# Wide cross attention in a Perceiver kernel: another order of the work of one batch

## The chip, the cores and the metric

The kernel runs on one core of a Trainium2 chip. The metric is device time in microseconds for one launch, the median of several executions. A batch is one of 32 independent rows of the input.

## What is computed

The program is a two-layer Perceiver. Its fourth stage, the one that changes, is the second cross attention: 64 latent queries of each of 32 batches attend to 1601 context rows with 16 heads of 16 dimensions.

```
q = (x @ Wq).reshape(B, N, 16, 16)          # B=32, N=64
k = (context @ Wk).reshape(B, M, 16, 16)    # M=1601, context dim 192
v = (context @ Wv).reshape(B, M, 16, 16)
scores = einsum('bhid,bhjd->bhij', q, k) * scale
scores = where(context_mask, scores, max_neg)
attn = softmax(scores)
out = einsum('bhij,bhjd->bhid', attn, v)
```

The output projection comes in the next stage.

## The kernel before

`wide_cross_attention` (L1550) computes keys and values of one batch from the transposed context in chunks, takes the row maxima of the scores in one pass, and in a second pass computes the scores again with keys on the partitions, exponentiates them and multiplies them with the values. Keys lie in 13 tiles of 124 (the last one shorter) and in four chunks of 4, 3, 3 and 3 tiles.

The work is a software pipeline over batches. In iteration n the rounds of `ROUNDS` (L1611) run in the order written there, and every engine walks the same list (`schedule`, L1641) and does its own part of each round. Rounds in `OF_B` work on batch n, those in `OF_NEXT` on batch n+2, `F1` and `F2` on batch n-1, all others on batch n+1. The first two and the last two batches are unrolled, and the loop between holds 28 batches. The rounds are:

- `K c`: key projection of chunk c, two halves of 5 matmuls (L1907). ScalarE rounds a copy to khi (L1831), VectorE copies the exact keys to kf (L2014).
- `V0 c`, `V1 c`: value projection of chunk c, up to two tiles each. ScalarE copies to val (L1859).
- `A c` (16 of them): rough scores for the maxima, two row-tiled matmuls (L1936) with a chunk's columns. VectorE adds the mask and takes the maximum (L2029).
- `mred`: VectorE joins the maxima and negates them (L2038 to L2041). `M`: TensorE transposes them (L1942), ScalarE copies them to augq (L1848).
- `B c` (13 of them): scores of key tile c, 12 row-tiled matmuls (L1956, L1959), which need augq. After every second tile ScalarE exponentiates two tiles (L1867). The score bank holds one pair, so an even tile waits for both exponentials of the pair before.
- `PV c`: 16 column-tiled matmuls (L1976) of the exponentials with the values into acc. `F0` copies acc to accs (ScalarE, L1873). `F1` multiplies accs by a selector (L1988), and ScalarE takes a logarithm and an exponential of the result for the reciprocal (L1877, L1879). `F2` multiplies and stores (L2047, stores at L1763).
- `Ln`, `X` on SyncE: loads of the context (L1727). `Sn`/`S`: ScalarE splits it (L1822, L1823). `Xn`/`X`: VectorE's rest (L2006 to L2008).
- `Q2`: VectorE scales the queries (qs, L2017). Behind this, SyncE loads the mask and the queries of the next batch, which is batch n+2 (L1731, L1736, 9 DMAs). `Qn`: ScalarE counts the mask with mcopy (L1837), GpSimd makes the mask's bias from the count. `Q1n`: ScalarE's rounded queries (L1842).

K, V, A, M and F1 share three PSUM banks, ring0 to ring2, in turn. `FILLS` (L1622) lists the fills in order of rounds, with 51 places; a fill waits until the one three places before it has been read by its last reader (`room`, L1887): for K that is VectorE's kf copy, for V ScalarE's, for A VectorE's maximum, for F1 the logarithm.

Of the kernel before, what the change touches and what calls it, by code (L numbers as in the profile page):

```python
# [378 lines left out]
def latent_cross_attention(nc, consts, ctx_x, ctxT, mask, g, b, WkvT, qT, klT, vl, oT):  # L379
# [15 lines left out]
    with ExitStack() as ctx:  # L395
# [65 lines left out]

        ROUNDS = [("R", 0), ("K", 1), ("Q", 0), ("B", 0), ("X", 3), ("RS", 1),
# [13 lines left out]
        FILLS = []  # L476
        for kind, c in ROUNDS:
            if kind in ("K", "Kn"):
# [21 lines left out]
        def schedule(engine_step, loop_engine, chain=None, per_round=0):  # L500

            def one(n, s):
                for kind, c in ROUNDS:
                    if kind in OF_B:
                        if there(n):
                            engine_step(kind, c, n, s % 6)
                    elif kind in OF_LAST:
                        if there(n - 1):
                            engine_step(kind, c, n - 1, (s + 5) % 6)
                    elif kind in OF_NEXT:  # L510
                        if there(n + 2):
                            engine_step(OF_NEXT[kind], c, n + 2, (s + 2) % 6)
                    elif there(n + 1):
                        engine_step(kind, c, n + 1, (s + 1) % 6)
# [1035 lines left out]
def wide_cross_attention(nc, consts, ctxT, mask, Wkv, qT, oT):  # L1550
# [17 lines left out]
    with ExitStack() as ctx:  # L1568
# [14 lines left out]
        kf = m.sbuf("kf", [128, 2, 2, W2])  # L1583
        val = m.sbuf("val", [128, 2, NKT, NH, VW])
# [11 lines left out]
        augq = m.sbuf("augq", [128, 2, 256], BF16)  # L1596
# [11 lines left out]
        sc = m.psum("sc", [128, 4, 512])  # L1608
        acc = m.psum("acc", [128, 256])

        ROUNDS = [("Ln", 0), ("Ln", 1), ("A", 0), ("B", 0), ("A", 1), ("B", 1), ("A", 2), ("X", 2), ("K", 1), ("F1", 0), ("PV", 0),  # L1611
# [6 lines left out]
        OF_B = ("B", "PV", "F0")  # L1618
        OF_NEXT = {"Ln": "L", "Sn": "S", "Xn": "X", "Kn": "K", "Qn": "Q", "Q1n": "Q1"}

        FILLS = []  # L1622
        turn = ROUNDS.index(("Kn", 0))
        for kind, c in ROUNDS[turn:] + ROUNDS[:turn]:
            if kind in ("Kn", "K"):
                FILLS += [(("K", c, o), "kf", 8, 2 * c + o, 0) for o in range(2)]
            elif kind == "V0":
                FILLS += [(("V", c, 0), "val", 8, 2 * c, 0)]
            elif kind == "V1":
                FILLS += [(("V", c, 1), "val", 8, 2 * c + 1, 0)]  # L1630
            elif kind == "A":
                FILLS += [((kind, c, o), "maxed", 32, 2 * c + o, 0) for o in range(2)]
            elif kind == "M":
                FILLS += [((kind, c, 0), "augq", 1, 0, -1)]
            elif kind == "F1":
                FILLS += [((kind, c, 0), "lden", 1, 0, -2)]
        while len(FILLS) % len(ring):
            FILLS.append(None)
        PLACE = {f[0]: n for n, f in enumerate(FILLS) if f}
# [1 line left out]
        def schedule(engine_step, loop_engine, chain=None, per_round=0):  # L1641

            def one(n, p, do_a, do_b, do_next, do_f):
                for kind, c in ROUNDS:
                    if kind in OF_B:
                        if do_b:
                            engine_step(kind, c, n, p)
                    elif kind in ("F1", "F2"):
                        if do_f:
                            engine_step(kind, c, n - 1, 1 - p)  # L1650
                    elif kind in OF_NEXT:
                        if do_next:
                            engine_step(OF_NEXT[kind], c, n + 2, p)
                    elif do_a:
                        engine_step(kind, c, n + 1, 1 - p)
# [909 lines left out]
def perceiver(nc, a, out):  # L2565

    N, D = a["x"].shape
    E = a["wg"].shape[1]
    slots = E * (int(N / E * 1.25) + 1)

    def scratch(name, shape):
        return nc.dram_tensor(name, shape, F32, kind="Internal").ap()
    qT, klT, oT0, q3T, oT3 = (scratch(name, (D, N)) for name in ("qT", "klT", "oT0", "q3T", "oT3"))
    vl, x2, x4, xn = (scratch(name, (N, D)) for name in ("vl", "x2", "x4", "xn"))
    logits = scratch("logits", (N, E))
    buf, ybuf = scratch("buf", (slots, D)), scratch("ybuf", (slots, D))

    latent_projections(nc, a, a["x"], a["ln_l_g"], a["ln_l_b"], a["qn_g"], a["kn_g"], a["WqT"], a["WlkvT"], qT, klT, vl)
    latent_cross_attention(nc, a, a["ctx"], a["ctxT"], a["mask0"], a["ln_x_g"], a["ln_x_b"], a["WkvT"], qT, klT, vl, oT0)
    gated_attention_and_ffn(nc, a, a["x"], oT0, a, x2, q3T)  # L2580
    wide_cross_attention(nc, a, a["ctxT"], a["mask1"], a["Wkv3"], q3T, oT3)
    laplacian_attention_and_router(nc, a, x2, oT3, a, x4, xn, logits, buf)
    routed_experts(nc, a, x4, xn, logits, a, buf, ybuf, out)
# [46 lines left out]
```

## Time and profile before

| | |
|---|---|
| median of 3 runs | 3820.42 us (3816.07 to 3820.52) |
| profiled execution | 3818.75 us, its span 3817.0 us |
| TensorE matmul | busy 3019.8 us, 79% |
| VectorE | busy 2548.8 us, 67% |
| ScalarE | busy 1931.1 us, 51% |
| GpSimd | busy 748.6 us, 20% |

The changed stage runs from about 1896 to 3282 us of the span. Times in the rows are microseconds from the start of the span, unless marked ns. A row of the order of time has start, duration (of several merged instructions together), engine, line, operation, what is written and read, count, and in brackets the idle time before it with what ended it. PE is TensorE, PEld its weight loads, DVE is VectorE, ACT is ScalarE, SPq the queue of SyncE. L12 is line 12 of the kernel.

### The profile page before, as it was taken

Reading aid. Unit: us, or ns where it says so; the run is one execution under the profiler, and the core shown is the slowest. Engines: PE = TensorE matmul, PEld = TensorE weight load, DVE = VectorE, ACT = ScalarE, POOL = GpSimd, SP = SyncE. Lnnn points to the kernel's source line nnn. Section 1 sums busy time; section 2 is a strip of 40 time slices with the busy share of each in tenths; the row PEclk is TensorE's granted clock in tenths of the full one; section 3 lists DMA queues with packets and bytes.
Section 4 is the critical chain, followed back from the end, with each engine's and each line's share of the span. In section 5 each row is a group of like instructions: output and inputs, shape, how many; then the busy total and the mean of one; then the engine's idle time right before and its main releaser. Section 6 shows DMA issues by size and latency. Waiting matters only on the chain. (4 is left out here: it accounts for less than half of the span.)

```text
span 3817.0 us, 103916 instructions
## 1 busy us (share of the span) xinstructions
PE 3019.8 (79%) x36990; PEld 2570.1 (67%) x36990; DVE 2548.8 (67%) x7485; ACT 1931.1 (51%) x4178; POOL 748.6 (20%) x836
## 2 busy tenths in 40 slices
PE   3449999999999985566379999999999999543674
PEld 3348888888888884444258788787888888432453
DVE  5568888888888854766567777776777777464000
ACT  1146666667666643333236666666666666321111
POOL 0223233332333310000132211211221221001001
PEclk7669999999999996777569999999999999765887
DMA  2123332323323302000111111111111111213411
GB/s 65 52 85 81 82 83 81 81 82 82 83 81 80 84 10 66 23 22 17 37 33 40 42 42 40 42 40 39 43 39 43 43 39 27 77 41 111 156 48 61
DMA packets 235455, 221.58 MB, mean 58 GB/s; under 512 B 69516, under 2 KB 228545, under 8 KB 234816
## 3 DMA queue, kind: packets, MB, share of 16 engines
q1 hardware_dynamic: 232896, 208.22, 19.4%
q0 software_dynamic: 2048, 6.68, 0.5%
q8 instruction: 304, 4.98, 0.5%
q14 instruction: 207, 1.70, 0.1%
HBM read 186.30 MB, written 28.39 MB: 56 GB/s over the span
## 5 line engine op out<-in xcount | busy, mean ns | idle before, releaser
L1867 ACT ACTIVATE xb_P<-xb_sc 124x1024 f32<-124x1024 f32 (+1 forms) x416 | 405.6, 1023 | 428.9 <-PE xb_sc L1959 428.9
L2029 DVE CUSTOM_DVE_ANT_0 xb_junk<-xb_ring,xb_mbias 128x372 bf16<-128x372 f32 (+2 forms) x1024 | 526.3, 571 | 102.9 <-PE xb_ring L1936 98.6
L1936 PE MATMUL xb_ring<-xb_khi,xb_qhi 32*128 32x372 f32 (+2 forms) x1024 | 405.5, 443 | 45.4 <-DVE xb_kf L2014 16.0
L879 PE MATMUL xa_acc<-xa_raw,xa_P 124*128 124x193 f32 x1664 | 315.6, 330 | 7.3 <-ACT xa_P L754 7.0
L1959 PE MATMUL xb_sc<-xb_qs,xb_kf 32*124 32x128 f32 x6656 | 317.3, 271 | 0.0
L2014 DVE COPY xb_kf<-xb_ring 128x372 f32<-128x372 f32 (+2 forms) x256 | 138.8, 572 | 244.8 <-ACT xb_khi L1831 239.8
L1907 PE MATMUL xb_ring<-xb_xst,xb_whi 128*128 128x372 f32 (+2 forms) x768 | 263.2, 370 | 43.6 <-DVE xb_xst L2008 38.0
L1907 PE MATMUL xb_ring<-xb_whi,xb_xst 128*124 128x256 f32 (+1 forms) x1248 | 286.4, 292 | 2.9 <-DVE xb_maxes L2029 0.4
L1936 PEld LDWEIGHTS xb_ring<-xb_khi,xb_qhi 32*128 32x128 f32 x1024 | 181.3, 185 | 153.1 <-DVE xb_maxes L2029 56.4
L1959 PEld LDWEIGHTS xb_sc<-xb_qs,xb_kf 32*124 32x124 f32 x6656 | 282.7, 182 | 0.0
L879 PEld LDWEIGHTS xa_acc<-xa_raw,xa_P 124*128 124x128 f32 x1664 | 266.4, 189 | 18.7 <-ACT xa_P L754 12.3
L1804 POOL TENSOR_SCALAR xb_augk<-xb_mask,xb_some 1x1602 bf16<-1x1602 uint8 x128 | 206.4, 1613 | 252.6 <-PE xb_sc L1959 236.0
L865 PE MATMUL xa_sc<-xa_qblk,xa_kT 128*124 128x128 f32 x1664 | 239.0, 272 | 0.0
L1976 PE MATMUL xb_acc<-xb_P,xb_val 124*17 124x64 f32 x13312 | 230.8, 220 | 4.2 <-ACT xb_P L1867 4.2
L1907 PEld LDWEIGHTS xb_ring<-xb_whi,xb_xst 128*124 128x124 f32 (+1 forms) x1248 | 216.8, 188 | 22.7 <-DVE xb_maxes L2029 15.9
L672 POOL CAST xa_kTr<-xa_kT 128x744 fp32r<-128x744 f32 (+1 forms) x128 | 109.9, 858 | 621.2 <-ACT xa_kT L740 621.2
L1976 PEld LDWEIGHTS xb_acc<-xb_P,xb_val 124*17 124x17 f32 x13312 | 190.7, 97 | 44.0 <-issue 15.7
L1907 PE MATMUL xb_ring<-xb_wlo,xb_xst 128*124 128x256 f32 (+1 forms) x832 | 218.3, 284 | 0.0
L865 PEld LDWEIGHTS xa_sc<-xa_qblk,xa_kT 128*124 128x124 f32 x1664 | 216.1, 187 | 0.1
L1956 PE MATMUL xb_sc<-xb_augq,xb_augk 32*124 32x256 bf16 (+1 forms) x1664 | 201.3, 303 | 1.6 <-ACT xb_P L1867 1.6
L1907 PEld LDWEIGHTS xb_ring<-xb_xst,xb_whi 128*128 128x128 f32 x768 | 146.5, 193 | 76.7 <-issue 43.0
L1907 PE MATMUL xb_ring<-xb_xst,xb_wlo 128*128 128x372 f32 (+2 forms) x512 | 180.2, 352 | 0.0
(430 smaller groups left out, 7720.8 us busy)
## 6 DMA issues: line engine op xcount, KB each, us to landing
xa_raw<-in_ctx SPq DMA_DIRECT2D x64, 279.0 KB
ex_w<-in_W SPq DMA_DIRECT2D x16, 1024.0 KB, 10.1
xa_raw<-in_ctx SPq DMA_DIRECT2D x32, 372.0 KB
xa_xTr<-in_ctxT SPq DMA_DIRECT2D x64, 186.0 KB, 2.5
xb_raw<-in_ctxT SPq DMA_DIRECT2D x64, 186.0 KB, 2.5
xa_xTr<-in_ctxT SPq DMA_DIRECT2D x32, 248.0 KB, 2.7
xb_raw<-in_ctxT SPq DMA_DIRECT2D x32, 248.0 KB
xa_mask<-in_mask SPq DMA_DIRECT2D x32, 200.1 KB, 5.3
```

What stands on the lines that cost most here:

```text
L672: nc.gpsimd.tensor_copy(kTr[:, c % 2, :, 0:W], kT[:, p, :, k0:k0 + W]).then_inc(sem("kTr"), 1)
L865: i = nc.tensor.matmul(s_[0:w, 256 * u + 128 * o:256 * u + 128 * o + 128], kt[:, o, :], qblk[:, t3, o, :], start=False, stop=True, skip_gr ...
L879: i = nc.tensor.matmul(acc[:, o, :], w, raw[0:KEYS, t3, t, :], start=t == 0 and o == 0, stop=t == NKT - 1, skip_group_check=True)
L1804: nc.gpsimd.tensor_scalar(augk[r:r + 1, p, :], mask8[r:r + 1, :], -1.0, some[r:r + 1, 1:2], ALU.add, ALU.mult).then_inc(sem("augk"), 1)
L1867: nc.scalar.activation(P[0:w, pbuf(t, p), :].rearrange("p (r n) -> p r n", r=4), sc[0:w, :, half], ACT.Exp).then_inc(sem("exped"), 1)
L1907: i = nc.tensor.matmul(out, l, r, start=k == 0, stop=k == 4)
L1936: i = nc.tensor.matmul(bank[:, 0:w], qhi[r, p, o, 128 * s:128 * s + 128], khi[r, p, o, k0:k0 + w], start=True, stop=True)
L1956: nc.tensor.matmul(sc[0:w, r, at:at + 256], augk[rows(r), p, keys], augq[rows(r), p, :], start=True, stop=True)
L1959: i = nc.tensor.matmul(sc[0:w, r, at + 128 * o:at + 128 * o + 128], kf[rows(r), p, o, keys], qs[rows(r), p, o, 128 * (r % 2):128 * (r % 2) ...
L1976: i = nc.tensor.matmul(acc[32 * j:32 * j + VW, 64 * g:64 * g + 64], val[0:w, p, c, h, :], P[0:w, pbuf(c, p), place(h):place(h) + 64], star ...
L2014: v.tensor_copy(kf[:, p, o, k0:k0 + w], ring[f % 3][:, 0:w]).then_inc(sem("kf"), 1)
L2029: v.tensor_tensor_reduce(out=junk[:, k, 0:w], in0=ring[f % 3][:, 0:w], in1=mbias[:, p, k0:k0 + w], scale=1.0, scalar=-3.0e38, op0=ALU.add, ...
```

## The change

The list `ROUNDS` is put in another order. It has the same rounds and no instruction is added or removed on any engine. In the new list A2, X2 and K1 stand between B1 and B2, nothing between B2 and B3, and A3 follows; most A rounds stand alone or in pairs between other rounds where they stood in groups of three; PV rounds stand singly in the first half; F1 stands ahead of A1; Q2 stands behind K3 instead of ahead of A5; Qn stands behind A14; mred and M stand ahead of Kn, and Sn2 is last. Since M and others now lie on the other side of the point where the list of fills begins (`turn`), the offsets in `FILLS`, which say of which batch a fill is relative to the others, are computed by a function `behind` instead of being written out.

```diff
-        ROUNDS = [("Ln", 0), ("Ln", 1), ("A", 0), ("B", 0), ("A", 1), ("B", 1), ("A", 2), ("X", 2), ("K", 1), ("F1", 0), ("PV", 0),
-                  ("A", 3), ("B", 2), ("A", 4), ("B", 3), ("S", 3), ("K", 2), ("V0", 0), ("F2", 0), ("Q2", 0), ("PV", 1), ("PV", 2),
-                  ("A", 5), ("B", 4), ("A", 6), ("B", 5), ("A", 7), ("X", 3), ("V1", 0), ("V0", 1), ("PV", 3), ("PV", 4),
-                  ("A", 8), ("B", 6), ("A", 9), ("B", 7), ("A", 10), ("Sn", 0), ("K", 3), ("V1", 1), ("Qn", 0), ("PV", 5), ("PV", 6),
-                  ("A", 11), ("B", 8), ("A", 12), ("B", 9), ("Xn", 0), ("Sn", 1), ("V0", 2), ("V1", 2), ("PV", 7), ("PV", 8),
-                  ("A", 13), ("B", 10), ("A", 14), ("B", 11), ("A", 15), ("Sn", 2), ("V0", 3), ("V1", 3), ("mred", 0), ("PV", 9), ("PV", 10),
-                  ("B", 12), ("Q1n", 0), ("Xn", 1), ("Kn", 0), ("M", 0), ("PV", 11), ("PV", 12), ("F0", 0)]
+        ROUNDS = [("Ln", 0), ("Ln", 1), ("A", 0), ("B", 0), ("F1", 0), ("A", 1), ("B", 1), ("A", 2), ("X", 2), ("K", 1), ("B", 2),
+                  ("B", 3), ("A", 3), ("K", 2), ("V0", 0), ("PV", 0), ("A", 4), ("PV", 1), ("S", 3), ("A", 5), ("B", 4), ("A", 6),
+                  ("PV", 2), ("A", 7), ("B", 5), ("PV", 3), ("A", 8), ("V1", 0), ("F2", 0), ("A", 9), ("B", 6), ("B", 7), ("X", 3),
+                  ("A", 10), ("V0", 1), ("PV", 4), ("Sn", 0), ("PV", 5), ("A", 11), ("K", 3), ("Q2", 0), ("Sn", 1), ("V1", 1), ("PV", 6),
+                  ("PV", 7), ("A", 12), ("B", 8), ("B", 9), ("A", 13), ("V0", 2), ("A", 14), ("Qn", 0), ("PV", 8), ("PV", 9), ("A", 15),
+                  ("B", 10), ("B", 11), ("V1", 2), ("V0", 3), ("V1", 3), ("Xn", 0), ("mred", 0), ("B", 12), ("PV", 10), ("Xn", 1),
+                  ("M", 0), ("Q1n", 0), ("Kn", 0), ("PV", 11), ("PV", 12), ("F0", 0), ("Sn", 2)]
...
-        for kind, c in ROUNDS[turn:] + ROUNDS[:turn]:
+
+        def behind(kind, n):
+
+            return (-2 if kind in OF_B else -3 if kind in ("F1", "F2") else 0 if kind in OF_NEXT else -1) + (n < turn)
+
+        for at in range(turn, turn + len(ROUNDS)):
+            kind, c = ROUNDS[at % len(ROUNDS)]
+            d = behind(kind, at % len(ROUNDS))
```

## Rows read from the trace of the kernel before

**Rows 1.** Stretches of TensorE: stretch, length, PE busy (count), clock, DMA, GB/s

```profile
2389.57:2430.87 41.30, 39.79 (x830) 1.00 0.15 41
2389.57:2392.89 3.32, 3.11 (x58) 1.00 0.02 5
2409.08:2411.69 2.61, 2.40 (x53) 1.00 0.11 22
2426.48:2427.17 0.69, 0.69 (x27) 1.00 0.00 0
```

**Rows 2.** Waits from 2300 to 3300: us in total, times, longest

```profile
PEld xb_ring L1936 <- DVE xb_maxes L2029: 39.0, 119, 0.6
PEld xb_ring L1936 <- DVE xb_kf L2014: 31.0, 87, 0.7
```

**Rows 3.** Order of time of TensorE in one batch

```profile
2400.47 0.28 PE L1907 MATMUL xb_ring<-xb_whi,xb_xst 128*124 128x256 f32 x1
...
2401.74 1.09 PE L1976 MATMUL xb_acc<-xb_P,xb_val 124*17 124x64 f32 x64
2402.76 0.61 PE L1936 MATMUL xb_ring<-xb_khi,xb_qhi 32*128 32x372 f32 x2
...
2410.30 0.43 PE L1936 MATMUL xb_ring<-xb_khi,xb_qhi 32*128 32x372 f32 x1 [0.18 <-DVE xb_maxes L2029]
...
2411.69 0.43 PE L1907 MATMUL xb_ring<-xb_xst,xb_whi 128*128 128x362 f32 x1
...
2413.46 0.28 PE L1907 MATMUL xb_ring<-xb_whi,xb_xst 128*124 128x256 f32 x1
...
2427.17 0.49 PE L1907 MATMUL xb_ring<-xb_xst,xb_whi 128*128 128x496 f32 x1
...
2429.53 0.38 PE L1942 MATMUL xb_ring<-xb_ident,xb_negmax 128*128 128x128 f32 x2
...
2430.87 0.70 PE L1936 MATMUL xb_ring<-xb_khi,xb_qhi 32*128 32x496 f32 x2
```

**Rows 4.** Order of time of VectorE in the same batch

```profile
2390.37 0.68 DVE L2029 CUSTOM_DVE_ANT_0 xb_junk<-xb_ring,xb_mbias 128x496 bf16<-128x496 f32 x1 [0.56 <-PE xb_ring L1936]
...
2394.06 0.54 DVE L2006 TENSOR_TENSOR xb_xst<-xb_raw,xb_xst 64x372 fp32r<-64x372 f32 x1
...
2395.74 1.00 DVE L2014 COPY xb_kf<-xb_ring 128x372 f32<-128x372 f32 x2
...
2403.13 0.48 DVE L2017 TENSOR_SCALAR xb_qs<-xb_qf,xb_some 128x512 f32<-128x512 f32 x1
...
2409.69 0.55 DVE L2029 CUSTOM_DVE_ANT_0 xb_junk<-xb_ring,xb_mbias 128x372 bf16<-128x372 f32 x1 [1.64 <-PE xb_ring L1936]
...
2410.16 0.54 DVE L2029 CUSTOM_DVE_ANT_0 xb_junk<-xb_ring,xb_mbias 128x372 bf16<-128x372 f32 x1
...
2424.89 0.17 DVE L2041 SCALAR_TENSOR_TENSOR xb_negmax<-xb_most,xb_neghi 128x8 f32<-128x8 f32 x1
```

**Rows 5.** Order of time of ScalarE in the same batch

```profile
2405.24 1.94 ACT L1867 ACTIVATE xb_P<-xb_sc 124x1024 f32<-124x1024 f32 x2 [2.54 <-PE xb_sc L1959]
...
2414.23 0.81 ACT L1831 ACTIVATE xb_khi<-xb_ring 128x362 fp32r<-128x362 f32 x2
...
2415.20 1.53 ACT L1837 ACTIVATE xb_mcopy<-xb_mask 128x1602 bf16<-128x1602 uint8 x1
```

**Rows 6.** SyncE's queue: query loads at the start, mask and queries in the loop

```profile
1904.85 3.70 SPq L1736 DMA_DIRECT2D xb_qf<-q3T  x8
...
2446.68 0.37 SPq L1731 DMA_DIRECT2D xb_mask<-in_mask  x1
2447.24 4.53 SPq L1736 DMA_DIRECT2D xb_qf<-q3T  x8
```

**Rows 7.** DMA issues from 2300 to 3300: count, size, median us to landing

```profile
xb_raw<-in_ctxT SPq DMA_DIRECT2D x44, 186.0 KB, 2.4
...
oT<-xb_o_sb SPq DMA_DIRECT2D x100, 16.0 KB, 1.5
```

More of the change, by code:

```diff
@@ L1623, in wide_cross_attention @@
         turn = ROUNDS.index(("Kn", 0))
-        for kind, c in ROUNDS[turn:] + ROUNDS[:turn]:
+        def behind(kind, n):
[3 more added lines that the diff above has]
+            d = behind(kind, at % len(ROUNDS))
             if kind in ("Kn", "K"):
-                FILLS += [(("K", c, o), "kf", 8, 2 * c + o, 0) for o in range(2)]
+                FILLS += [(("K", c, o), "kf", 8, 2 * c + o, d) for o in range(2)]
             elif kind == "V0":
-                FILLS += [(("V", c, 0), "val", 8, 2 * c, 0)]
+                FILLS += [(("V", c, 0), "val", 8, 2 * c, d)]
             elif kind == "V1":
-                FILLS += [(("V", c, 1), "val", 8, 2 * c + 1, 0)]
+                FILLS += [(("V", c, 1), "val", 8, 2 * c + 1, d)]
             elif kind == "A":
-                FILLS += [((kind, c, o), "maxed", 32, 2 * c + o, 0) for o in range(2)]
+                FILLS += [((kind, c, o), "maxed", 32, 2 * c + o, d) for o in range(2)]
             elif kind == "M":
-                FILLS += [((kind, c, 0), "augq", 1, 0, -1)]
+                FILLS += [((kind, c, 0), "augq", 1, 0, d)]
             elif kind == "F1":
-                FILLS += [((kind, c, 0), "lden", 1, 0, -2)]
+                FILLS += [((kind, c, 0), "lden", 1, 0, d)]
         while len(FILLS) % len(ring):
```

## The prediction, made before the change was run

> **What bounds the kernel now.** The change touches one stage of six. The first view to read is the table of stretches: one batch of this stage, from the first maxima matmul of one batch to that of the next, takes 41.30 us and TensorE is counted busy for 39.79 us of it, at a granted clock of 1.00, the 2.4 GHz level [rows 1]. So TensorE, which walks the hand-written order, sets the period; the clock has nothing left to give. The second view is the list of waits: in 1000 us the weight loads waited 39.0 us for the maxima (VectorE L2029) and 31.0 us for the key copies (L2014) [rows 2]. Both are waits for one of the three ring banks. The third view is the order of time on TensorE. A8 begins at 2409.08 [rows 1], the second matmul of A9 has to wait until 2410.30 and K3 starts only at 2411.69 [rows 3]: this group of three A and two B rounds takes 2.61 us [rows 1]. VectorE explains it: its first reduction starts at 2409.69, the second at 2410.16, so one follows each 0.47 us [rows 4], and the fourth, which frees K3's bank, is over at about 2411.6. Three A rounds in a burst want 2.8 us of VectorE and TensorE has far less to do meanwhile. The group A0 to A2 with its 496 columns takes 3.32 us for the same reason [rows 1]. A lone B takes 0.69 us [rows 1]. If A costs 0.3 us and B 0.6 us unstalled, a group of 3 A and 2 B would need 2.1 us, so some 0.5 to 1.2 us of each such group is stall (there are six a batch, of which the rows show two): 3 to 5 us a batch is the most that any order can win here. It is more than the 1.5 us of idle time in the table, because a stalled pair of matmuls runs one behind the other and is counted busy.
>
> **The steps that cost nothing or little.** No instruction is added or removed; all is order. M with its copy goes ahead of K0: two transposes of 0.38 us together [rows 3], whose negated maxima are ready if VectorE has passed A15, X0 and the reduction; between A15 and M TensorE now has B10, B11, V12, V03, V13, B12 and PV10, about 5 us, against some 4 us on VectorE (two reductions 0.9; X0, 2.2, which is X2's 1.68 [rows 4] at 496 columns; the maxima's four small operations, of which the last took 0.17 [rows 4], 0.8). Cost nothing; if the cover failed, below 0.5 us. F1 goes ahead of A1, and A2 now waits for its bank until ScalarE took the logarithm; behind F1 stand A1 and B1, and that covers it. Sn2 goes behind F0: its 0.8 us of ScalarE lies in a place where it idled, and its reader X2 comes 5 us later. S3, Sn0, Sn1 and both Xn are moved among copies that have a microsecond of slack; Sn1 now stands ahead of V11's copy and waits about 0.2 us for V11's matmuls, with only that copy behind it. On SyncE the stores of F2 stay behind X2's loads, and X3's two loads now run before Q2's nine instead of behind them. GpSimd's chain hangs on ScalarE's Q and on the last B round, and has half a batch of slack.
>
> **The maxima.** I walk the new order with the old durations, t from A0, each A's second matmul and each next ring user waiting for the bank three places back. Durations: a reduction 0.47 us (0.6 at 496 columns), first one 0.6 to 0.8 us after its matmul, X2 1.68, a key copy 0.5 [rows 1, 3, 4]; K 1.8 (K3 took 1.77), V00 1.27, two PV 1.02, K0 2.36 [rows 3]; an isolated A 0.35 (not shown; bounds: 0.2, a bare pair of passes, and 0.46, A10 to K3 with a wait in it [rows 3]; I take the middle); F1 0.6, an estimate from M, whose two matmuls are half as wide. A0, B0, F1 to 1.8; A1 to 2.15, B1; A2 2.7 and, waiting, 3.3; K1 3.9 to 5.6; B2, B3 to 6.75. Here is the stall that stays: VectorE needs 0.8 + six reductions to 5.0, then X2 to 6.7, then K1's copies to 7.7, so A3 is held until 7.3 and K2 until 7.8. K2 to 9.6, V00 to 10.8, PV0, A4, PV1 to 12.2; A5 (0.4 of waiting), B4, A6 (0.4), PV2, A7, B5, PV3 to 15.7; A8, V10 to 17.35; A9, B6, B7, A10, V01 to 20.3; PV4, PV5 to 21.35; A11 (0.35 of waiting, behind X3), K3 21.95 to 23.65. Before, K3 ended 23.89 us after A0 (2413.46 less 2389.57) [rows 1, 3], with PV5 and A11 (0.9 us) still to come. Gain to this point: 1.1 us.
>
> From there on, stalls are few: V11, PV6, PV7, A12 to A13 with B8 and B9, V02, A14, PV8, PV9, A15 with B10 and B11, V12, V03, V13 end at about 34.1. Then B12 0.69 [rows 1], PV10 0.51, M 0.32 (1.34 from M to A0 less two PV), K0 2.36, PV11 and PV12 1.02 [rows 3]: 4.9 us, so A0 would follow at 39.0, a gain of 2.3 us a batch.
>
> **The load that comes due.** Q2 is the step that I think decides. On VectorE it scales the queries (L2017, 0.48 us [rows 4]); then SyncE may load the mask and the queries of the batch after next, nine DMAs, and ScalarE's mcopy (Qn, L1837, 1.53 us [rows 5]) waits for them. Before, Q2 ended at 2403.6 and mcopy began at 2415.20 [rows 4, 5], 11.6 us later, with no wait on a DMA. Now Q2 stands behind K3's copies and Qn between A14 and PV8. K3's last copy chain: half of 0.81 on ScalarE, half of 1.00 on VectorE, with hand-overs and 0.48 for the scaling, ends at t = 25.2 [rows 4, 5]. From there: 0.25 us to SyncE, 0.37 + 0.2 for the mask's issue, the eight query issues, which took 3.70 us when the queue was fresh and 4.53 behind the stores [rows 6] (I take 4.1 less the last one's 0.3), and the landing, 1.5 us (the stores) to 2.4 (the loads) [rows 7], taken as 2.1: 6.7 us. The load is there at t = 31.9; ScalarE reaches Qn at about 29.9 (B9 ends at 27.3, two exponentials 1.94 [rows 5], V02's copy 0.5). Behind the waiting mcopy on ScalarE stand the exponentials of tiles 10 and 11 and the copies of V12, V03 and V13; behind those, on TensorE, B12 (it needs the score bank), M and K0. So: 31.9 + 1.65 (mcopy and its read) + 1.94 for two exponentials [rows 5] = 35.5, + 0.1, B12 at 35.6 instead of 34.1, + 4.9 = 40.5.
>
> The Trainium skill (DMA: Bandwidth & Descriptors, the anatomy of one DMA) gives a DMA about 2.0 us of fixed time. The loads' 2.4 and the stores' 1.5 lie around it; with 2.0 the sum would be 40.4.
>
> **The sum.** 41.3 - 40.5 = 0.8 us a batch; the loop has 28 batches and the unrolled ends hold about 2 more that gain, so 30 x 0.8 = 24 us. The profiled execution took 3818.75 us (span 3817.0 and 1.75 around it), 1.7 under the median 3820.42. From the profiled one 3794.7, from the median 3796.4: I say 3796.
>
> **Rivals.** (a) The load is in time, or ScalarE reaches Qn later anyway: period 39.0, 30 x 2.3 = 69 us, 3751. For it: the estimate of t = 29.9 leaves only 2 us; against: it needs a landing at once after the issues. (b) Slower: the load chain takes over, longer than I think. With the issues of the old places (4.5) and a landing of 2.4 the load is at +7.5, and the more frequent switches add 0.7 us ahead of K3: 40.5 + 0.8 + 0.7 = 42.0, + 0.7 x 30 = 21 us, 3841. It is slower from the point where Q2 to mcopy takes more than 7.5 us with the walk as it is, and each tenth beyond goes one for one into the period. For it: the chain has no cover left; against: the stores no longer crowd the issues. (c) The maxima are not spread where it matters: the cluster A0 to A3 with X2 and both key copies stays VectorE's, A's taken out from beside B cost TensorE time that B hid; the period stays within 0.25 us of 41.3, 3813 to 3828.
>
> **Chances and range.** Forecast case (period 39.8 to 41.05) 0.45, (a) 0.15, (b) 0.23, (c) 0.17. Faster by over 0.2% (0.2%, 7.6 us, is about what a measurement of this kernel can tell from no change): 0.60; within: 0.17; slower: 0.23. The range reaches from about (a), 3752, to about (b), 3838.
>
> **What the profile after would show.** A period near 40.5 between first maxima matmuls; ScalarE's mcopy waiting about 2 us for the query load in every batch, and B12 and the exponentials 10 and 11 late behind it; waits of weight loads on L2029 nearly halved; waits on L2014 before A3 and K2. If mcopy never waits for a DMA, my deciding step is wrong and (a) should be seen; if waits on L2029 don't fall, (c). A period over 41.5 with a wait at mcopy would be (b).

## The result, and the profile after

| | before | after |
|---|---|---|
| median of 4 | 3820.47 us (3816.07 to 3820.64) | 3856.52 us (3851.71 to 3869.1) |
| ratio | | 1.0102, 95% interval 1.0076 to 1.0128 |
| profiled span | 3817.0 us | 3857.4 us |

The changed kernel is 36 us slower, where 24 us faster was forecast. (Two executions of later runs lasted several times as long as the others of their kernel, 15184.67 us with X0 late and 8948.93 us with the score tiles apart; the ratios leave them out.) The loss lies in the changed stage. I cut the stage at ScalarE's copy of the finished sums (accs, L1873 before, L1880 after), once a batch. Before, 28 batches of the steady part (without the one in which the loop turns) last 40.89 to 41.35 us, 41.05 on average. After, they fall into two kinds. These are stretches of the changed kernel, each one batch (length, TensorE busy, count, granted clock, DMA, GB/s):

```profile
2358.82:2400.07 41.25, 38.85 (x819) 1.00 0.19 44
2400.07:2443.13 43.06, 40.41 (x819) 0.96 0.16 39
2443.13:2487.78 44.65, 41.41 (x819) 0.92 0.16 38
2487.78:2528.54 40.76, 38.87 (x819) 1.00 0.16 42
```

Sixteen of the 28 batches have a mean clock of 1.00 and last 40.6 to 41.9 us, 41.13 on average. The other twelve have 0.92 or 0.96 and last 44.05 on average, 3.0 us more than a batch before. Twelve times 3.0 us is 36 us, nearly the whole difference. (The two batches behind the loop add 1.9 us.) In the fast kind TensorE is busy for 38.9 us a batch, 0.8 less than the 39.7 of a batch before that is cut the same way, so the new order did pack TensorE's work more tightly; it then waited the gain away.

Where it waits, from the list of waits of the changed kernel, 2300 to 3300 (us in total, times, longest), which answers to [rows 2]:

```profile
ACT xb_mcopy L1844 <- DMA xb_qf<-q3T: 72.9, 23, 4.1
PEld xb_sc L1963 <- ACT xb_P L1874: 61.5, 27, 3.5
...
PEld xb_ring L1943 <- DVE xb_maxes L2036: 15.9, 61, 0.7
...
PEld xb_ring L1943 <- DVE xb_kf L2021: 7.0, 22, 0.3
```

The waits of the A rounds for maxima and key copies went from 39.0 and 31.0 us to 15.9 and 7.0: that part of the change does what it says. The waits of the K and V rounds for maxima hardly fell, from 28.2 us to 25.7. In their place came a wait of mcopy for the query load in every batch, and a wait of the score tiles (B12) for exponentials. The order of time shows the chain in one batch, first SyncE, then ScalarE, then TensorE:

```profile
2425.79 0.38 SPq L1738 DMA_DIRECT2D xb_mask<-in_mask  x1
2426.38 5.32 SPq L1743 DMA_DIRECT2D xb_qf<-q3T  x8
```

```profile
2433.02 1.54 ACT L1844 ACTIVATE xb_mcopy<-xb_mask 128x1602 bf16<-128x1602 uint8 x1 [3.32 <-DMA xb_qf<-q3T]
2434.47 0.19 ACT L1844 ACTIVATION_READ_ACCUMULATOR xb_mcopy<-xb_mask 128x1 f32 x1
2434.56 1.92 ACT L1874 ACTIVATE xb_P<-xb_sc 124x1024 f32<-124x1024 f32 x2
```

```profile
2436.53 0.32 PE L1963 MATMUL xb_sc<-xb_augq,xb_augk 32*113 32x256 bf16 x4 [2.46 <-ACT xb_P L1874]
...
2438.45 0.62 PE L1914 MATMUL xb_ring<-xb_xst,xb_wlo 128*128 128x496 f32 x1
```

Q2 ends at 2425.52, the last of the eight query loads is issued at 2431.7, mcopy starts at 2433.02, the two exponentials behind it end at 2436.48 and B12 starts. TensorE has been idle for 2.46 us. From two microseconds later on K0's matmuls take 0.41 us from start to start instead of the 0.23 that the same ones took before. The clock says why (stretches inside that batch):

```profile
2400.07:2433.79 33.72, 33.53 (x689) 1.00 0.13 30
2436.53:2438.45 1.92, 1.92 (x55) 0.91 0.40 105
2438.45:2441.34 2.89, 2.89 (x8) 0.50 0.14 35
2441.34:2443.13 1.79, 1.79 (x69) 0.95 0.00 0
```

After 33.7 us of nearly gapless work at 1.00, the gap of 2.46 us ahead of B12 (the last matmul of V13 starts at 2433.79, B12 at 2436.53) is followed by a stretch at 0.50, that is 1.2 GHz for 2.4. It catches K0, the densest work of the batch. In the six batches with a mean clock of 0.96 the clock is down for some 3 us, in the six with 0.92 for some 7.

### The profile page after: what moved, and what is told of

It reads as the page before. It is cut to its first block and busy times, and to the rows that moved or that the text cites. A ratio compares the mean times of both kernels' runs of the same rounds, so it can differ in the third digit from the quotient of the medians.

```text
span 3857.4 us, 103974 instructions
## 1 busy us (share of the span) xinstructions
PE 3034.7 (79%) x36990; PEld 2569.4 (67%) x36990; DVE 2558.3 (66%) x7485; ACT 1953.5 (51%) x4178; POOL 759.0 (20%) x836
## 5 line engine op out<-in xcount | busy, mean ns | idle before, releaser
L2036 DVE CUSTOM_DVE_ANT_0 xb_junk<-xb_ring,xb_mbias 128x372 bf16<-128x372 f32 (+2 forms) x1024 | 540.7, 572 | 179.1 <-PE xb_ring L1943 177.1
L1943 PE MATMUL xb_ring<-xb_khi,xb_qhi 32*128 32x372 f32 (+2 forms) x1024 | 309.7, 444 | 10.7 <-issue 5.0
L1914 PE MATMUL xb_ring<-xb_xst,xb_whi 128*128 128x372 f32 (+2 forms) x768 | 274.9, 386 | 42.8 <-DVE xb_xst L2015 38.0
L1966 PE MATMUL xb_sc<-xb_qs,xb_kf 32*124 32x128 f32 x6656 | 286.7, 273 | 0.0
L1966 PEld LDWEIGHTS xb_sc<-xb_qs,xb_kf 32*124 32x124 f32 x6656 | 260.5, 184 | 0.0
L1983 PE MATMUL xb_acc<-xb_P,xb_val 124*17 124x64 f32 x13312 | 246.1, 222 | 1.8 <-ACT xb_P L1874 1.7
L1963 PE MATMUL xb_sc<-xb_augq,xb_augk 32*124 32x256 bf16 (+1 forms) x1664 | 183.8, 294 | 76.9 <-ACT xb_P L1874 76.9
L1796 POOL TENSOR_SCALAR xb_some<-xb_count 128x1 f32<-128x1 f32 x32 | 9.6, 300 | 1015.2 <-ACT xb_mcopy L1844 1015.2
L1914 PEld LDWEIGHTS xb_ring<-xb_xst,xb_whi 128*128 128x128 f32 x768 | 154.9, 204 | 77.2 <-issue 49.2
L1943 PEld LDWEIGHTS xb_ring<-xb_khi,xb_qhi 32*128 32x128 f32 x1024 | 137.8, 184 | 94.5 <-DVE xb_maxes L2036 23.2
```

Of the source, the lines that this page charges most:

```text
L1914: i = nc.tensor.matmul(out, l, r, start=k == 0, stop=k == 4)
L1943: i = nc.tensor.matmul(bank[:, 0:w], qhi[r, p, o, 128 * s:128 * s + 128], khi[r, p, o, k0:k0 + w], start=True, stop=True)
L1963: nc.tensor.matmul(sc[0:w, r, at:at + 256], augk[rows(r), p, keys], augq[rows(r), p, :], start=True, stop=True)
L1966: i = nc.tensor.matmul(sc[0:w, r, at + 128 * o:at + 128 * o + 128], kf[rows(r), p, o, keys], qs[rows(r), p, o, 128 * (r % 2):128 * (r % 2) ...
L1983: i = nc.tensor.matmul(acc[32 * j:32 * j + VW, 64 * g:64 * g + 64], val[0:w, p, c, h, :], P[0:w, pbuf(c, p), place(h):place(h) + 64], star ...
L2036: v.tensor_tensor_reduce(out=junk[:, k, 0:w], in0=ring[f % 3][:, 0:w], in1=mbias[:, p, k0:k0 + w], scale=1.0, scalar=-3.0e38, op0=ALU.add, ...
```

## Experiments: the late load

Two theories stood first. L: the late load holds mcopy, mcopy holds the exponentials and B12, and the clock falls in some of the gaps. O: the new order itself costs, through its more frequent changes between full and tiled matmuls and through A rounds no longer hidden beside B.

**Load early.** The changed order with Q2 moved back:

```
-  ... ("K", 2), ("V0", 0), ("PV", 0), ... ("K", 3), ("Q2", 0), ("Sn", 1), ...
+  ... ("K", 2), ("V0", 0), ("Q2", 0), ("PV", 0), ... ("K", 3), ("Sn", 1), ...
```

> The changed order with one round moved back: Q2 stands behind V0 0 and ahead of PV0, some 15 us earlier, so SyncE loads mask and queries long before mcopy asks for them. Theory L (the late load holds mcopy, that holds the exponentials 10 and 11 and so B12, and TensorE's clock falls in some of those gaps): mcopy no longer waits for a DMA, no wait before B12, clock 1.00 in every batch but the loop's turn, period 39.0 to 39.6 us, time 3765 to 3785 us. Rival O (the new order itself costs, through more changes between full and tiled matmuls and through maxima that B rounds no longer hide): period stays at 41 us or more, time 3815 us or more, even with the waits gone.

Measured: 3945.98 us, ratio 1.0335 (1.0318 to 1.0352). L's range is missed; the time lies where O has it, but not for O's reason, as the runs below show. mcopy no longer waits for a DMA, as L has it, and yet a batch takes 45.55 us on average. The waits (2300 to 3300) are new ones:

```profile
PEld xb_ring L1943 <- DVE xb_kf L2021: 50.5, 26, 2.5
...
PEld xb_ring L1949 <- DVE xb_negmax L2048: 37.2, 21, 1.8
```

The clock is below 1.00 in 25 of the 28 batches; the other three, with waits that are 0.7 to 0.9 us shorter, last 42.4 us on average. So about half of the 4.5 us that a batch is longer than before is the clock's. TensorE now waits for VectorE, for the negated maxima ahead of M and for K0's copy. VectorE is not overloaded; single operations last too long. Its order of time at the end of a batch, and GpSimd's beside it:

```profile
2425.72 0.67 DVE L2013 TENSOR_TENSOR xb_xst<-xb_raw,xb_xst 64x496 fp32r<-64x496 f32 x1
2426.40 0.67 DVE L2014 TENSOR_TENSOR xb_xst<-xb_raw,xb_xst 64x496 fp32r<-64x496 f32 x1
2427.08 1.98 DVE L2015 TENSOR_TENSOR xb_xst<-xb_raw,xb_xst 64x496 fp32r<-64x496 f32 x1
2429.09 0.19 DVE L2045 TENSOR_REDUCE xb_most<-xb_maxes 128x8 f32<-128x32 f32 x1
2429.32 1.37 DVE L2046 TENSOR_SCALAR xb_neghi<-xb_most 128x8 bf16<-128x8 f32 x1
...
2431.00 1.83 DVE L2013 TENSOR_TENSOR xb_xst<-xb_raw,xb_xst 64x372 fp32r<-64x372 f32 x1
2432.84 1.85 DVE L2014 TENSOR_TENSOR xb_xst<-xb_raw,xb_xst 64x372 fp32r<-64x372 f32 x1
2434.71 1.86 DVE L2015 TENSOR_TENSOR xb_xst<-xb_raw,xb_xst 64x372 fp32r<-64x372 f32 x1
```

```profile
2426.71 1.83 POOL L1803 TENSOR_SCALAR xb_mbias<-xb_mask,xb_some 128x1602 bf16<-128x1602 uint8 x1 [0.25 <-POOL xb_some L1797]
2429.06 1.60 POOL L1811 TENSOR_SCALAR xb_augk<-xb_mask,xb_some 1x1602 bf16<-1x1602 uint8 x1 [0.52 <-PE xb_sc L1966]
2430.83 1.61 POOL L1811 TENSOR_SCALAR xb_augk<-xb_mask,xb_some 1x1602 bf16<-1x1602 uint8 x1 [0.17 <-POOL xb_augk L1811]
2432.61 1.69 POOL L1811 TENSOR_SCALAR xb_augk<-xb_mask,xb_some 1x1602 bf16<-1x1602 uint8 x1 [0.17 <-POOL xb_augk L1811]
2434.47 1.71 POOL L1811 TENSOR_SCALAR xb_augk<-xb_mask,xb_some 1x1602 bf16<-1x1602 uint8 x1 [0.17 <-POOL xb_augk L1811]
```

An X operation takes 0.54 us alone ([rows 4]) and 1.85 while GpSimd runs its mask passes, and it ends each time with a pass: one VectorE operation, one GpSimd pass, in turns. Even an operation on 8 columns takes 1.37 us. A new theory, P: these VectorE operations and GpSimd's passes exclude each other for a whole instruction, and in the changed order they meet, unless mcopy is late and holds GpSimd back too. The Trainium skill (SBUF — State Buffer, "SBUF: two separate sides") states that rule: VectorE and GpSimd have one pair of SBUF ports in common as an exclusive lock, which a `tensor_tensor` with two SBUF inputs (against a GpSimd instruction that reads SBUF) or a scalar operation in its faster mode needs. The traces agree: the operations that read PSUM keep their length. In the kernel before, 135 reductions of 496 columns and 56 key copies ran during a pass, and they took 0.67 us, as the others do.

**mcopy later.** The load stays where the change put it, and mcopy goes behind B12:

```
-  ... ("A", 14), ("Qn", 0), ("PV", 8), ... ("B", 12), ("PV", 10), ...
+  ... ("A", 14), ("PV", 8), ... ("B", 12), ("Qn", 0), ("PV", 10), ...
```

> The changed order with the load where the change put it, but with Qn (mcopy) moved from behind A14 to behind B12, so that the exponentials 10 and 11 and three value copies go ahead of the waiting mcopy on ScalarE. Theory L: what hurts is what is queued behind mcopy, so B12 waits no more; mcopy itself waits little; period 39.2 to 40.0 us, time 3770 to 3795 us. Rival O: 41 us or more, 3815 us or more.

Measured: 3866.4 us, ratio 1.0128 (1.0111 to 1.0145). B12 no longer waits, which is L's part, but the time is not won. P explains the larger part: with mcopy behind B12 the bias pass and the augk passes come one after another, and the operations of L2014 with 372 columns take 1168 ns on average, which is 0.54 for X2's and 1.86 for X1's; TensorE waits 41.3 us in 1000 for K0's copy. Another 31.7 us it waits for M's copy to augq, which on ScalarE now stands behind mcopy. And in 13 of 28 batches the clock is at 0.96: these last 43.35 us, the other 15 41.89, with the same waits in both. Both repairs of the load run into GpSimd's passes.

**Filling the gap.** To part the clock from the gap, TensorE is given work in it, which writes columns of acc's bank that nobody reads (acc is made 512 columns wide for it):

```
+                    if c == NKT - 1:
+                        ...
+                        for _ in range(4):
+                            nc.tensor.matmul(acc[:, 256:512], ident[:], w_raw[:, 0, 0:256], start=False, stop=True, ...)
```

> The changed order with four extra matmuls ahead of each B12 (128 x 128 by 256 columns, fp32, into unused columns of acc's bank, read by nobody; about 2.1 us), which lie in the gap that TensorE has there anyway. It parts the gap from the clock. Theory L with the clock as the larger part: granted clock 1.00 in nearly all batches, periods of 43 to 45 us gone, all at 40.6 to 41.3 us, time 3808 to 3825 us in spite of more work. If the clock is innocent (the slow batches are slow because their load is late): time stays at 3850 us or rises.

Measured: 3839.99 us, ratio 1.0068 (1.0048 to 1.0087): 16.5 us less than the changed kernel, with 128 more matmuls. The two intervals still overlap; the batches tell the two apart more clearly. The clock reads 1.00 in both long stretches of the stage (2020 to 2640 and 2700 to 3200), no batch of the 28 has a lowered clock where the changed kernel has twelve, and no batch but the one of the loop's turn is longer than 42.4 us. So the clock is not a companion of the slow batches but costs by itself. The size was missed by 15 us: the batches last 41.7 us and not 41.0, since the load is as late as before (7.6 us from Q2's end to mcopy, on average) and B12 still waits for the exponentials (34.9 us in 1000).

**The two moves in the old order.**

```
-  ... ("F2", 0), ("Q2", 0), ... ("V1", 1), ("Qn", 0), ... ("B", 9), ("Xn", 0), ... ("A", 14), ("B", 11), ...
+  ... ("F2", 0), ... ("V1", 1), ... ("B", 9), ("Q2", 0), ("Xn", 0), ... ("A", 14), ("Qn", 0), ("B", 11), ...
```

> The order of before with only two rounds moved: Q2 from behind F2 to behind B9, Qn from behind V1 1 to behind A14. No maxima are spread. Theory L: the load is there some 7 us after Q2, at about 36 us into the batch, mcopy waits 3 to 4 us, B12 is 2.5 to 3 us late; the period goes from 41.0 to about 44 us where the clock holds and 45 to 47 us where it falls; time 3900 to 3960 us. Rival O: the two moves cost nothing by themselves, time 3815 to 3825 us.

Measured: 3944.22 us, ratio 1.0336 (1.0319 to 1.0354), most batches at 44.3 to 45.4 us, four of them at 46.2 to 47.0, and mcopy waits 92.4 us in 22 batches for the query load. Within the range of L. The clock is below 1.00 in 25 of 28 batches, which last 45.1 us on average; the other three last 43.5. TensorE waits for the exponentials already at a PV round here (L1976, 51.6 us in 1000). No maxima are spread and the tiling changes are as before: the late load with mcopy behind it makes this kernel slow by itself.

## Experiments: VectorE and GpSimd

**X0 late in the old order.** This is P by itself, with nothing else of the change:

```
-  ... ("B", 9), ("Xn", 0), ("Sn", 1), ... ("V1", 3), ("mred", 0), ...
+  ... ("B", 9), ("Sn", 1), ... ("V1", 3), ("Xn", 0), ("mred", 0), ...
```

> The order of before with one round moved: Xn0 from behind B9 to behind V1 3, where the changed order has it. Theory P: X0 (2 us) now comes between A15 and mred, so X1 starts 2 us later and falls under augk, which starts at B12; its three operations take about 1.8 us each instead of 0.54, K0's copies and A1 are late; period 43 to 44 us, time 3880 to 3920 us. Without such a collision X0's move costs nothing, as VectorE has 2.8 us of idle time before K0's copies: 3815 to 3825 us.

Measured: 3904.39 us, ratio 1.0223 (1.0203 to 1.0243), a batch 43.92 us. Operations of VectorE by form, 2300 to 3200 (busy us, mean ns):

```profile
L2007 DVE TENSOR_TENSOR xb_xst<-xb_raw,xb_xst 64x372 fp32r<-64x372 f32 x40 | 47.8, 1196 | 0.5
L2008 DVE TENSOR_TENSOR xb_xst<-xb_raw,xb_xst 64x372 fp32r<-64x372 f32 x40 | 47.8, 1196 | 0.5
```

Half of these 40 are X2, which is free; 1196 ns on average is 0.54 for them and 1.85 for X1. A0 now waits 1.3 us for K0's copy, where it did not wait before, and behind that wait the clock falls. First the wait, from the order of time of TensorE, then the stretches behind it:

```profile
2420.89 0.98 PE L1936 MATMUL xb_ring<-xb_khi,xb_qhi 32*128 32x496 f32 x2 [1.35 <-DVE xb_kf L2014]
```

```profile
2420.89:2422.93 2.04, 2.00 (x42) 1.00 0.56 147
2422.93:2429.76 6.83, 6.83 (x61) 0.50 0.16 42
```

It does so in 24 of the 28 batches, which last 44.19 us on average; the other four last 42.32. One round, moved by 7 us, costs 2.9 us a batch, though VectorE had idle time of its own to put it in: 1.3 us of that are there at full clock, the rest is the clock.

**Shorter passes.** The run with the load early, its four augk passes cut to 402 of 1602 columns. The mask rows keep their initial 1 in the other columns there, so part of the scores is shifted; that part of the computation is left out.

```
-  nc.gpsimd.tensor_scalar(augk[r:r + 1, p, :], mask8[r:r + 1, :], ...)
+  nc.gpsimd.tensor_scalar(augk[r:r + 1, p, 0:402], mask8[r:r + 1, 0:402], ...)
```

> The run q2_early with its order untouched, but GpSimd's four augk passes cover 402 of 1602 columns (the mask of this input is all ones, so the other columns keep their zero). Theory P: a pass takes some 0.4 us instead of 1.6, so an X1 operation is held less, about 0.7 us instead of 1.18 on average, A0 and F1 wait little for K0's copy; period 40 to 41.5 us, time 3790 to 3840 us, against 3946 us. If VectorE is late for another reason than GpSimd's passes: time stays near 3946 us.

Measured: 3783.85 us, ratio 0.9915 (0.9898 to 0.9931), below the expected range, every steady batch 39.6 to 40.0 us and at a clock of 1.00. From 3946 to 3784 us by an engine that is busy 20% of the time. (The expectation says that the other columns are zero; they are 1, as above.)

**VectorE's work moved away from GpSimd's.**

```
-  ("A", 13), ("V0", 2), ("A", 14), ("Qn", 0), ... ("A", 15), ... ("V1", 3), ("Xn", 0), ("mred", 0), ("B", 12), ("PV", 10), ("Xn", 1), ...
+  ("A", 13), ("Xn", 0), ("V0", 2), ("A", 14), ("Xn", 1), ("Qn", 0), ... ("A", 15), ("mred", 0), ... ("V1", 3), ("B", 12), ("PV", 10), ...
```

> The run q2_early (load early, 3946 us) with VectorE's SBUF work taken out from under GpSimd: Xn0 behind A13, Xn1 behind A14, mred right behind A15, so that all of it is over before GpSimd starts mbias and augk. Theory P (with the load early, GpSimd's mask passes run while VectorE has X0, the maxima's small operations and X1 to do, and each of these VectorE operations is held until a GpSimd pass ends): each 372-column X operation back at 0.54 us, no wait of M for negmax, no wait of A0 or F1 for K0's copy, clock 1.00, period 39.0 to 39.8 us, time 3765 to 3790 us. Rival O (the new order costs by its many changes between full and tiled matmuls): 41 us or more, 3815 us or more.

Measured: 3878.58 us, ratio 1.0157 (1.014 to 1.0174). Better than 3946 by 67 us, and negmax and K0's copy are in time, but 89 us above the forecast range. X0 and X1 now stand between the reductions of A13 to A15, where TensorE waits for each of them; VectorE's, GpSimd's and TensorE's order of time:

```profile
2449.09 1.85 DVE L2015 TENSOR_TENSOR xb_xst<-xb_raw,xb_xst 64x372 fp32r<-64x372 f32 x1
```

```profile
2448.85 1.70 POOL L1803 TENSOR_SCALAR xb_mbias<-xb_mask,xb_some 128x1602 bf16<-128x1602 uint8 x1 [0.25 <-POOL xb_some L1797]
```

```profile
2451.57 0.38 PE L1914 MATMUL xb_ring<-xb_whi,xb_xst 128*124 128x256 f32 x1 [1.73 <-DVE xb_maxes L2036]
```

The last X1 operation meets mbias, the reductions of A15 come behind it, and V12 waits 1.73 us for their bank. Behind it the clock is at 0.96 in 16 of 28 batches (43.58 us; the other twelve last 41.94). I had placed the work by GpSimd's passes and had forgotten the bursts of the maxima, which the change was to undo.

**M behind Kn again**, on top of that run: `("M", 0), ("Q1n", 0), ("Kn", 0)` becomes `("Q1n", 0), ("Kn", 0), ("M", 0)`.

> The run q2_x_early with M behind Kn again, as in the order of before. It prices the part of the change that puts the maxima's transposes ahead of the key projection. Theory: B0 needs M's copy and K0 has 2.4 us of slack behind it, so the place of M is worth nothing by itself: within 5 us of q2_x_early. Rival: M ahead of K0 is what makes the new order good, as its copy is off ScalarE's queue ahead of the key copies: 10 to 30 us slower than q2_x_early.

Measured: 3884.0 us, ratio 1.018 (1.0163 to 1.0197) against 1.0157: 5.4 us slower with overlapping intervals. The place of M is worth about 5 us here, which the intervals do not tell from nothing, and not the 10 to 30 us of the rival.

**One pass in place of four.** The load early, and GpSimd computes all rows of augk at once, with a scale and an offset for each row (gain, two operations on one column a batch, from row masks set once, not shown here):

```
-                    for k in range(4):
-                        r = 32 * k
-                        nc.gpsimd.tensor_scalar(augk[r:r + 1, p, :], mask8[r:r + 1, :], -1.0, some[r:r + 1, 1:2], ALU.add, ALU.mult)...
+                    nc.gpsimd.tensor_scalar(augk[:, p, :], mask8[:], gain[:, 0:1], gain[:, 1:2], ALU.mult, ALU.add)...
```

> The run q2_early (changed order, load early, 3946 us) with GpSimd's four augk passes over one row each replaced by a single pass over all 128 rows, with two small operations that prepare its scale and offset; nothing of the computation is left out. Theory P (VectorE's X and maxima operations are held by GpSimd's passes): the pass of 1.6 us can hold one or two of them, not five; period 39.6 to 40.3 us as in q2_early_short (39.65), time 3783 to 3805 us, clock 1.00. If the number of passes doesn't matter: near 3946 us.

Measured: 3775.04 us, ratio 0.9894 (0.9877 to 0.9911): 43 us faster than before, 81 us faster than the change as it was made. A steady batch takes 39.54 us, and this one stretch, free of the loop's turn, is two fifths of the stage (length, busy time and count of PE, PEld, DVE, ACT and POOL, clock, DMA, GB/s):

```profile
2700.00:3200.00 500.00, 492.72 (x10319) 408.68 (x10319) 403.83 (x1143) 340.50 (x550) 69.37 (x72) 1.00 0.16 40
```

TensorE is busy for 98.5% of it, the clock is 1.00 and GpSimd is busy for 69.37 us, against 101.19 in the kernel before and 63.78 in the short run. Of the five VectorE operations that were held, two are left. One of those freed is of X0: the two small operations ahead of mbias let it start later, so not all of the gain is the number of passes. Rival O, that the tiling changes and the A rounds apart from B cost the gain, is out: this kernel has them all, and a batch takes 39.54 us.

**The single pass without the rest.** It could be that GpSimd's shorter work is the gain and the order nothing.

> The order of before with the single augk pass. Theory: in that order X1 is over before GpSimd starts augk, and only X0's first operation is held (by mbias, which stays), so the four passes cost it nothing but the key copies' little: 3808 to 3822 us. Rival: the gain of q2_early_short over before comes from GpSimd's shorter work and not from the order: 3780 to 3795 us here too.

Measured: 3817.58 us, ratio 0.9997 (0.9987 to 1.0007). In the old order the single pass is worth nothing. The edit is the same one, on the kernel before.

> The changed order as it is (Q2 late) with the single augk pass. Theory L: the late load still holds mcopy and B12, and TensorE's clock still falls in some batches, so 3835 to 3856 us. Rival: GpSimd's passes are the whole loss of the changed order, and the load's lateness is hidden: 3783 to 3805 us.

Measured: 3850.03 us, ratio 1.0099 (1.0078 to 1.012). In the changed order with the late load it is worth about nothing either (3856.52 without it). The X1 operations are back at 0.54 us, and the batches are again of two kinds, 20 of 40.7 to 42.2 us and 8, with the clock lowered, of 42.9 to 44.8. So the loss of the change as it was made is the load's and the clock's; the lock comes out only when the load is repaired.

**The first four score tiles apart.** From the best kernel:

```
-  ... ("K", 1), ("B", 2), ("B", 3), ("A", 3), ("K", 2), ("V0", 0), ...
+  ... ("K", 1), ("A", 3), ("B", 2), ("K", 2), ("B", 3), ("V0", 0), ...
```

> The run one_pass with the first four score tiles no longer close: A3 goes ahead of B2, and K2 comes between B2 and B3. Theory: B2 and B3 ahead of A3 are what TensorE does while VectorE works off X2 and K1's copies; without them A3 and K2 wait longer, 0.5 to 1 us a batch: 15 to 30 us slower than one_pass. Rival: the place of the score tiles costs nothing: within 5 us of one_pass.

Measured: 3821.5 us, ratio 1.0005 (0.9995 to 1.0015), 46 us slower than one_pass; the direction is as expected, the size half as large again as the upper end. The weight load of A3's second matmul, first in the best kernel, then in this one:

```profile
2339.32 0.18 PEld L1962 LDWEIGHTS xb_ring<-xb_khi,xb_qhi 32*128 32x128 f32 x1 [0.33 <-DVE xb_kf L2040]
```

```profile
2316.23 0.18 PEld L1962 LDWEIGHTS xb_ring<-xb_khi,xb_qhi 32*128 32x128 f32 x1 [1.37 <-DVE xb_kf L2040]
```

It waits 1.37 us for K1's copy where B2 and B3 left 0.33 of waiting. That is 1.04 of the 1.55 us that a batch gets longer, and so on average over the 28 batches (1.38 against 0.34). This one cluster carries as much as the whole gain of the best kernel.

## Why the prediction was wrong, point by point

- **The maxima.** Right in kind and nearly in size. The walk put K3 at t = 21.95 and the end of Q2 at 25.2; the trace has 22.2 (2422.12 less 2399.93) and 25.6. The waits of the A rounds on L2029 fell by more than half. Without the late load the walk's period was 39.0 us; the best kernel, whose order differs from the walk's in Q2 alone, has 39.54.
- **The base.** I took 41.30 us from one pair of A0's [rows 1]; cut at accs, 28 batches average 41.05. The forecast gain was too large by 0.25 us a batch, 7 us in all.
- **The load that comes due.** The mechanism was right and its length 10% short: from the end of Q2 to mcopy 6.5 to 8.7 us, 7.5 on average over 28 batches, where 6.7 stands in the prediction. The eight issues took 3.9 to 6.2 us, 4.9 on average (5.32 in the batch shown), not 4.1. As the prediction says, each tenth goes one for one into the period: in the sixteen batches at full clock the length of a batch less its time from Q2 to mcopy is 34.05 us on average (33.98 to 34.28), where the prediction's sum has 33.8. With 7.5 us in place of 6.7 its own sum comes to 41.3: this term alone takes the forecast gain away.
- **The step that failed** is the sentence "the clock has nothing left to give", with the price at nothing of what the clock can lose. I computed a stall of 1.5 us on TensorE at B12 and priced it as 1.5 us. The stalls were 1.5 to 3.7 us, and behind twelve of them the clock went to 1.2 GHz for some 3 or some 7 us of the densest work. Those twelve batches are 2.9 us longer than the other sixteen, but 0.9 of it is their later load; by the 34.05 us above, the lowered clock costs 1.5 us in each of the six at 0.96 and 2.6 in each of the six at 0.92, 25 us in all. It was not the only miss. Without it the batches would average 41.5 us, against 41.05 before, and the kernel would still be some 13 us slower. (The sixteen at full clock average 41.13, but they are those whose load came early, so they do not stand for all.) Together, the forecast gain of 0.8 us a batch became a loss of 1.3: of these 2.1 us the clock makes 0.9, the longer load 0.75, the walk 0.25 and the base 0.25. Rival (b), slower, had the sign, the wait and the load's 7.5 us right, but not the rest: it asked for 0.7 us of tiling switches, and neither the 34.05 us here nor one_pass leaves room for them.
- **The tiling switches.** Ten more a batch, put at up to 1.0 us. The best kernel has the same 31 switches and takes 0.5 us more than the walk, which counted none of them. Of that, 0.4 us is a wait of M for the negated maxima. If the walk is right otherwise, the ten cost less than 0.5 us; no run changes the switches alone, so their price stays open. (The Trainium skill, TensorEngine Tiling (Array Packing), Key Properties, states that a switch drains TensorE, without a price.)
- **GpSimd.** "Has half a batch of slack" was true of when its results are due and blind to what its passes do to VectorE meanwhile. It did no harm to the change as made, where the late mcopy held GpSimd back (its batches and those of the run with the single pass are alike 34.05 and 34.04 us long at full clock, less the time from Q2 to mcopy), but it is why rival (a), the load in time, would have been 3946 us and not 3751. The trace of before showed it, had I asked for VectorE's operations by form, 2300 to 3200 of the kernel before:

```profile
L2006 DVE TENSOR_TENSOR xb_xst<-xb_raw,xb_xst 64x496 fp32r<-64x496 f32 x21 | 38.9, 1851 | 0.7
...
L2007 DVE TENSOR_TENSOR xb_xst<-xb_raw,xb_xst 64x496 fp32r<-64x496 f32 x21 | 14.1, 671 | 0.3
```

The same operation takes 671 ns on one line and 1851 on the line ahead of it: the first one meets mbias in every batch.

## What to carry to other kernels

In a hand-written order, list for each moved round what it starts on other queues (here nine DMAs behind one VectorE operation) and when their result is asked for; it is the distance between the two rounds that must hold, not their places. A gap on TensorE is priced with what the clock takes from the work behind it, and whoever moves VectorE's SBUF work or GpSimd's must lay the two lists side by side, for they exclude each other even where neither is busy. A reordering may need its partner: here the order was worth 43 us only with the load early and GpSimd's four passes made one, and either repair alone was worth nothing or less. And a wait must be priced in every batch: the batches that happened to escape the clock's fall are not the kernel without it.

## What the runs showed of the hardware that I had not expected

- TensorE's granted clock, at 1.00 through 33.7 us of work, stood at 0.50 some 2 us after a gap of 2.46 us, with B12, PV10 and M between. In the steady batches of this trace, waits ahead of B12 of 1.5 to 2.06 us were followed by none of it, those of 2.92 to 3.65 us always, and of those between, some were and some were not. The length of the gap does not tell it alone: in the old order with X0 late, waits of 1.3 to 1.6 us ahead of A0 were followed by a lowered clock in 24 of 28 batches. What parts the cases stays open. The Trainium skill (TensorE: Matmul & The Clock Gate, Part 1) describes a clock gate that halves the clock after idleness; the rows agree on the two levels. A filler of 1.9 us in the gap kept the clock in all 28 batches.
- A VectorE operation on 8 columns, 0.17 us alone, took 1.37 us beside a GpSimd pass over a single row, and such passes of 1.6 us stretched a row of three X operations from 1.6 to 5.6 us. A pass over 1602 columns takes 1.60 us for one row and 1.68 for 128 where VectorE leaves it alone (the single pass in the old order), so one pass for all rows costs about a quarter of four. In the best kernel it takes 2.37 us in most batches, so the holding goes both ways.
